# A macaron block on one core: row maxima five groups ahead instead of six, padded transposes later in their group, one first load of x

## The reference

```
x = x + 0.5 * ffn(layernorm(x))      # silu(x Wu^T) * (x Wg^T), then Wd^T; the three weights ternary
x = x + attn(layernorm(x))           # q, k, v with biases; causal softmax over 256 keys
x = x + 0.5 * ffn(layernorm(x))
```

## Time and profile before

| | us |
|---|---|
| runs | 593.73, 595.56, 595.39 (median 595.39) |
| the profiled execution, its own time | 593.51 |
| its span, first to last instruction | 591.8 |
| attention in it | about 200 to 424 |

### The profile page before, as it was taken

The page is one execution under the profiler, slowest core; times in us unless marked ns, Lnnn a source line. Parts: engine busy times, 40 slices in busy tenths (PEclk is TensorE's granted clock), DMA queues, the critical chain, the costliest instruction groups (busy, mean ns, idle before and its releaser), DMA issues.

```text
span 591.8 us, 12391 instructions
## 1 busy us (share of the span) xinstructions
PE 561.4 (95%) x4244; PEld 343.8 (58%) x4244; DVE 480.7 (81%) x1861; ACT 400.6 (68%) x717; POOL 169.3 (29%) x263
## 2 busy tenths in 40 slices
PE   2889999999999989999999999997999999999998
PEld 2345565655666755666566656554455665665566
DVE  5898978989875889898989897996797688756654
ACT  4857665674655378797888878886666665674642
POOL 3115201101530035454545454656401101100100
PEclk9999999999999999999999999999999999999999
DMA  8711101100105151423323323212201212111112
GB/s 297 229 34 37 18 19 37 36 19 19 37 18 126 39 112 56 93 78 71 88 64 101 76 74 84 66 50 39 37 1 35 64 45 69 39 55 54 35 37 72
DMA packets 72238, 37.90 MB, mean 64 GB/s; under 512 B 35536, under 2 KB 71632, under 8 KB 72144
## 3 DMA queue, kind: packets, MB, share of 16 engines
q1 hardware_dynamic: 72176, 37.11, 24.3%
HBM read 18.22 MB, written 10.49 MB: 49 GB/s over the span
## 4 chain that ended last, share of the span: by engine, by line
PE 71%; DVE 15%; DMA 4%; ACT 2%; issue 2%; SPq 2%; POOL 2%; DVEq 0%; ACTq 0%; POOLq 0%
PE bank L1163 33%; PE bank L1175 17%; DVE sm_out L980 6%; PE bank L1262 5%; PE bank L1319 4%; PE bank L1289 4%; PE bank L1330 4%; DMA q_st<-mx_hl 3%; PE bank L1335 2%; PE bank L1344 2%; DVE hid L849 1%; POOL xn L408 1%; DMA x<-in_x_dram 1%; DVE hl L864 1%; DVE stats L728 1%
## 5 line engine op out<-in xcount | busy, mean ns | idle before, releaser
L980 DVE CUSTOM_DVE_ANT_0 sm_out<-bank,mask 128x256 f16<-128x256 f32 (+1 forms) x512 | 151.3, 352 | 18.4 <-PE bank L1289 17.6
L481 ACT ACTIVATE silu<-bank,w_scale 128x512 f32<-128x512 f32 x128 | 87.3, 683 | 113.0 <-PE bank L1163 113.0
L849 DVE SCALAR_TENSOR_TENSOR hid<-silu,h_unit,bank 128x512 f32<-128x512 f32 x128 | 95.0, 743 | 63.8 <-ACT silu L481 63.5
L1175 PE MATMUL bank<-wT_down,hh 128*128 128x256 f16 x512 | 118.3, 273 | 2.5 <-DVE hl L864 2.3
L1175 PE MATMUL bank<-wT_down,hl 128*128 128x256 f16 x512 | 118.2, 273 | 0.0
L1163 PE MATMUL bank<-xh,wT_up 128*128 128x512 f16 x256 | 98.0, 383 | 1.0 <-DVE xl L793 0.7
L864 DVE TENSOR_TENSOR hl<-hid,hh 128x512 f16<-128x512 f32 x128 | 98.5, 770 | 0.0
L1163 PE MATMUL bank<-xh,wT_gate 128*128 128x512 f16 x256 | 97.3, 380 | 1.1 <-DVE hid L849 1.1
L1163 PE MATMUL bank<-xl,wT_up 128*128 128x512 f16 x256 | 98.0, 383 | 0.0
L1163 PE MATMUL bank<-xl,wT_gate 128*128 128x512 f16 x256 | 97.3, 380 | 0.0
L417 POOL TENSOR_TENSOR xnl<-xn,xnh 128x1024 f16<-128x1024 f32 x13 | 28.3, 2177 | 213.2 <-ACT xn L520 177.8
(11 more groups left out here) (133 smaller groups left out, 790.4 us busy)
## 6 DMA issues: line engine op xcount, KB each, us to landing
q_st<-q_scratch SPq DMA_DIRECT2D x32, 256.0 KB
q_scratch<-q_hl SPq DMA_DIRECT2D x16, 256.0 KB, 2.2
out_dram<-x SPq DMA_DIRECT2D x7, 512.0 KB, 3.0
x<-in_x_dram SPq DMA_DIRECT2D x1, 3072.0 KB, 15.5
k_scratch<-k_hl SPq DMA_DIRECT2D x16, 128.0 KB, 2.4
k_st<-k_scratch SPq DMA_DIRECT2D x16, 128.0 KB
shared<-in_w_up_t_dram SPq DMA_DIRECT2D x2, 512.0 KB, 6.7
shared<-in_w_gate_t_dram SPq DMA_DIRECT2D x2, 512.0 KB, 8.3
```

Source lines behind the costliest of these rows:

```text
L481: act.activation(silu[:, e % 2, :], U[e % 2][:, :], ACT.Silu, scale=w_scale[:, 0:1]).then_inc(silu_ready, 1)
L849: dve.scalar_tensor_tensor(out=hid[:, e % 4, :], in0=silu[:, e % 2, :], scalar=h_unit[:, 0:1], in1=GT[e % 2][:, :], op0=ALU.mult, op1=ALU. ...
L980: ins = dve.tensor_tensor_reduce(sm_out[:, i, cols], SM[i][:, cols], mask[:, S - size:S], -1.0 / MAX_UNIT, -MASKED, ALU.add, ALU.min, rowm ...
L1175: ins = pe.matmul(ACC[t % 2][:, 0:D], part[:, par, e, t * P:(t + 1) * P], wT_down[:, e, :], start=(e == 0 and part is hh), stop=(e == NE - ...
```

## The change

1. The lead is n + 5 where it was n + 6, on PE and on DVE. Before the loop, one group of row maxima fewer is made; in the last pair, one more.
2. `mx_q` is padded from 32 to 128 columns a half and cleared once at the start, and the transpose's stationary operand and its result are 128 wide. The copy reads the same 32 rows as before.
3. `max_transposes` moves from behind part 0 of `scores` to just ahead of part 2; `max_copy` from behind part 0 of `exps` to between parts 1 and 2; `max_parts` from ahead of `causal` to behind it.
4. Part 0 of `scores` of the groups 9, 17, 25, 33, 41, 49 and 57 (`n % 8 == 1`) is made one step early, ahead of `output_transposes`.
5. x's first chunk is loaded in one transfer instead of two.

```diff
-        mx_q = sb("mx_q", [P, 2, 2, HH, QT], F16)
+        mx_q = sb("mx_q", [P, 2, P], F16)
+        mx_parts = mx_q[:, :, 0:2 * HH * QT].rearrange("p n (a h t) -> p n a h t", a=2, h=HH)
-        MT = PV[0:2 * QT * HH, 0:P // 2].bitcast(F16)
+        MT = PV[:, 0:P // 2].bitcast(F16)
+        def begun_early(n):
+            return 2 < n < NG - 2 and n % 8 == 1
@@ sync
-            for half in range(2):
-                tiles = slice(half * TT // 2, (half + 1) * TT // 2)
-                sp.dma_start(x[:, tiles, :], x_dram[:, tiles, :]).then_inc(ld_x0[half], 16)
+            sp.dma_start(x[:, 0:TT, :], x_dram[:, 0:TT, :]).then_inc(ld_x0, 16)
@@ gpsimd, in attention_pair
-                        if g in (0, 2) and not end:
-                            max_parts(b + 1, g // 2)
                         if odd and g in (2, 3):
                             add_output(b - 1, g - 2, 3 - g)
                         if not (end and g == 3):
                             causal(4 * b + g + 1)
+                        if g in (0, 2) and not end:
+                            max_parts(b + 1, g // 2)
@@ scalar, in attention_pair
                             exps(n + 1, range(0, 1))
-                        if g % 2 and not end:
-                            max_copy(b + 1, g // 2)
                         if not last:
...
-                            exps(n + 1, range(1, 3))
+                            exps(n + 1, range(1, 2))
+                        if g % 2 and not end:
+                            max_copy(b + 1, g // 2)
+                        if not (end and g == 3):
+                            exps(n + 1, range(2, 3))
@@ vector
-                        lead = (4 * b + g + 6, (k + (g + 6) // 4) % 2, (g + 2) % 4)
-                        ahead = not (last and (k == 3 or (k == 2 and g >= 2)))
+                        lead = (4 * b + g + 5, (k + (g + 5) // 4) % 2, (g + 1) % 4)
+                        ahead = not (last and (k == 3 or (k == 2 and g == 3)))
...
-                for n in (4, 5):
-                    first_row_max(n)
-                row_max(6, 1, 2, 0)
+                first_row_max(4)
+                row_max(5, 1, 1, 0)
@@ tensor, in attention_pair
-                        if not (end and g == 3):
+                        if not (end and g == 3) and not begun_early(n + 1):
                             scores(*following, range(0, 1))
-                        if g % 2 and not end:
-                            pe.wait_ge(oT_ready, n)
-                            max_transposes(b + 1, g // 2)
...
                         projection(2)
+                        if g % 2 and not end:
+                            pe.wait_ge(oT_ready, n)
+                            max_transposes(b + 1, g // 2)
...
                             if not end:
-                                max_scores(n + 7, k + 2, 2, range(0, 1))
+                                max_scores(n + 6, k + 2, 1, range(0, 1))
+                                scores(*second, range(0, 1))
                             output_transposes(b, k, 0, (onorm_ready, 2 * b + 2))
@@ tensor, in attention
-                max_scores(5, 1, 1)
-                max_scores(6, 1, 2, range(0, 1))
+                max_scores(5, 1, 1, range(0, 1))
```

More of the change, by code:

```diff
@@ L133, in macaron_block @@
         LAST_ST = [SM[1], ST[0], ST[1]]
-        MT = PV[0:2 * QT * HH, 0:P // 2].bitcast(F16)
-        FIRST_MT = ST[0][0:2 * QT * HH, 0:P // 2].bitcast(F16)
+        MT = PV[:, 0:P // 2].bitcast(F16)
+        FIRST_MT = ST[0][:, 0:P // 2].bitcast(F16)
         ld_w = [[sem(f"ld_w{m}{half}") for half in range(2)] for m in range(3)]
-        ld_x0 = [sem(f"ld_x0{half}") for half in range(2)]
-        ld_x1, ld_xr = sem("ld_x1"), sem("ld_xr")
+        ld_x0, ld_x1, ld_xr = sem("ld_x0"), sem("ld_x1"), sem("ld_xr")
         xn_tile = sem("xn_tile")
@@ L346, in _ @@
             step(pool.tensor_copy(ident16[:, :], ident32[:, :]))
+            step(pool.memset(mx_q[:, :, :].bitcast(U32), 0))
             pool.memset(ones[:, :], 1.0).then_inc(const_ready, 1)
@@ L373, in max_parts @@
                 heads = rowmax[:, b % 2, :, half * HH:(half + 1) * HH].rearrange("p t h -> p h t")
-                pool.tensor_copy(mx_q[:, half, 0, :, :], heads).then_inc(mxhi_ready, 1)
+                pool.tensor_copy(mx_parts[:, half, 0, :, :], heads).then_inc(mxhi_ready, 1)
                 pool.wait_ge(mxhi_ready, 2 * b + half + 1)
-                pool.tensor_tensor(mx_q[:, half, 1, :, :], heads, mx_q[:, half, 0, :, :],
+                pool.tensor_tensor(mx_parts[:, half, 1, :, :], heads, mx_parts[:, half, 0, :, :],
                                    ALU.subtract).then_inc(mxlo_ready, 1)
@@ L583, in max_copy @@
                 maxima = FIRST_MT if b + half == 0 else MT
-                act.activation(mx_hl[:, half, :], maxima, ACT.Copy).then_inc(mx_ready, 1)
+                act.activation(mx_hl[:, half, :], maxima[0:2 * QT * HH, :], ACT.Copy).then_inc(mx_ready, 1)
             def exps(n, parts):
@@ L776, in ln_first @@
             def ln_first():
-                for half in range(2):
-                    dve.wait_ge(ld_x0[half], 16)
-                    ln_stats_of(0, range(half * TT // 2, (half + 1) * TT // 2))
+                dve.wait_ge(ld_x0, 16)
+                ln_stats_of(0, range(TT))
                 ln_moments(0)
@@ L1078, in attention_pair @@
                         if not (last and k == 3):
-                            row_max(4 * b + 10, (k + 2) % 2, 2, 0)
+                            row_max(4 * b + 9, (k + 2) % 2, 1, 0)
                         normalise(b, 0, 0)
@@ L1298, in max_transposes @@
                     pe.wait_ge(mx_ready, 2 * b + half)
-                pe.transpose(MT if b + half else FIRST_MT, mx_q[:, half, :, :, :].rearrange("p a h t -> p (a h t)"),
+                pe.transpose(MT if b + half else FIRST_MT, mx_q[:, half, :],
                              ident16[:, :]).then_inc(mxT_ready, 1)
@@ L1356, in attention_pair @@
                         n, end = 4 * b + g, last and k == 3
-                        lead = (n + 6, k + (g + 6) // 4, (g + 2) % 4)
-                        ahead = not (end or (last and k == 2 and g >= 2))
+                        lead = (n + 5, k + (g + 5) // 4, (g + 1) % 4)
+                        ahead = not (end or (last and k == 2 and g == 3))
                         def projection(place):
@@ L1363, in projection @@
                                 project(c + 2, at // 4, at % 4)
+                        second = (n + 2, b + (g + 2) // 4, k + (g + 2) // 4, (g + 2) % 4)
                         following = (n + 1, b + (g + 1) // 4, k + (g + 1) // 4, (g + 1) % 4)
                         if ahead:
-                            if g == 2:
+                            if g == 3:
                                 pe.wait_ge(st_loaded[1 - par][odd], 16 * N_ST * (pair + par + 1))
```

## The result

The changed kernel takes **609.38 us** (median of 4 runs, 607.93 to 610.57) against 595.45 for the kernel before in the same comparison: ratio 1.0237, 95% interval 1.0209 to 1.0265. It is slower, as forecast, but by 13.9 us where 6.6 was forecast (602 against 595.4), and outside the range of 590.5 to 607.

What follows compares the result with a forecast made beforehand. PE, DVE and ACT were taken as near full and tied by semaphores, DVE then transfers deciding even chunks, PE odd ones. -2.0 - 0.3 + 7.5 + 3.0 = +8.2 gave 602 us; own range 598.5 to 606, whole range 590.5 to 607.

Steps and rivals of the forecast that it cites:

- The prologue: Before the loop: one group of row maxima fewer lets the loop begin earlier, -2.0 us, between 0 and -2.2.
- The start: First load of x: one issue fewer sends the second chunk earlier, -0.3 us, between 0 and -0.5.
- The padding: At PE's 31 max transposes: the wider shape saves PE time but outputs then wait for ACT's copy, 0 us.
- what PE saves it waits: At the padded transposes: outputs wait for ACT's copy, so PE's saving from padding counts as 0.
- The copy, by its four places: The later ACT copy delays outputs in an odd chunk by 0.3, 0.5, 1.0 and 0.3 us.
- the 0.63 that the boundary was to hold: At an odd chunk's boundary: PE's 0.63 us of slack absorbs that much, leaving +2.0 of 2.6.
- The step that failed: Even chunks: only delay before DVE's gapless stretch, 0.3, and 0.2 at its other end count: +0.5 us each.
- The parts behind the masks: At g = 3 of an odd sequence: the transpose waits for POOL's later parts, +0.5 us, between 0 and 1.0.
- The last pair: Without projections PE reaches the waits sooner; a later load of maxima and later outputs cost +3.0 us, between 0 and 4.
- Early scores: At seven boundaries: scores begun early fill PE's wait for the results' copy, 0 us, at best -0.3 each.
- the wait for the copy is hidden: Rival for the late copy's places: its delays vanish, so the kernel is faster, 588.0 or 589.9 us; chance 0.17.
- under 0.7 us: Condition of the hidden-wait rival: it decides if an odd chunk's delay is under 0.7 us.

Runs made afterwards that it cites:

- the three small edits: Padded transposes, one first transfer of x and scores begun early; together, alone in the kernel before: 592.31 us, ratio 0.9953.
- the kernel with all three late places: The kernel before, lead still six, with the transposes, ACT's copy and POOL's parts at the changed kernel's late places: 611.69 us, ratio 1.0290.
- 631.8: The kernel before with only POOL's max_parts moved behind add_output and causal, transposes and copy early, lead six: 631.84 us, ratio 1.0625.
- 616.3: The changed kernel with POOL's max_parts put back ahead of add_output and causal, lead of five and late transposes and copy kept: 616.27 us, ratio 1.0363.
- 603.5: The changed kernel with ACT's copy ahead of part 1 of exps, still behind query_high, transposes left late: 603.46 us, ratio 1.0152.

## Why the prediction was right in sign and too small

From kernel to kernel the medians go +11.2 (copy), +0.4 (transposes), +6.0 (parts), -1.4 (the three small edits, from 611.69 to 610.28) and -0.9 (lead), together the 15.2 from 594.18 to 609.38 (13.9 against the 595.45 of its own comparison); the last two steps compare kernels that ran in different comparisons. In the profiles the difference of 17.0 was forecast as 8.2: -2.3 up to the first `outputs` (forecast -2.3), +4.9 for the three even chunks (forecast +1.5), +7.6 for the three odd ones (+6.0), +6.8 for the last pair (+3.0). Step by step:

- *The prologue, -2.0.* Right where it was read: the first x transposes at 210.0 against 212.1 with a lead of six, 2.1. But in the end only 0.9 is left in the medians. The group left out comes back in the last pair, where the prediction had DVE waiting: the first two `outputs` of the last chunk begin at 419.4 and 426.1 in after, at 421.0 and 426.9 with a lead of six, so that 2.1 became 1.6 and then 0.7. The chain of after runs over DVE there, through the row maxima of one group more, to the `scores` that wait for them (with a lead of six DVE is done with its maxima at 423.5, and the chain passes over PE):

```profile
423.91 0.20 DVE sm_out L984
424.11 0.02 DVE rowmax L984
424.13 0.14 issue
424.26 0.39 PE bank L1322
```

  These are single executions. Among kernels that are the same up to that point, the first `outputs` stand between 217.0 and 218.3, so tenths of such a difference mean little.
- *The start, -0.3.* Mechanism right. The statistics start 0.53 earlier in the profile; the whole kernel gains 0.8, with an interval from -0.2 to -1.4 that holds the forecast.
- *The padding, 0.* Wrong: it gives 2.0, or 1.4 at equal clock, with the places early. That 2.4 had been expected from 0.2 at four places of three odd chunks is near by luck, since the profile has the gain at one place of every chunk. So "what PE saves it waits" is not what happens. With the late places and a lead of six the small edits make the chunks 0.2 shorter too (29.9 for 30.1); what the padding alone gives there was not measured. The Trainium skill (TensorEngine Tiling (Array Packing), section Key Properties) says that a change of tiling mode drains TensorE. The traces agree as far as they go: PE's weight load stood at the narrow transpose for 9.5 us in 31, at the padded one for 2.2 in 5. Only a fraction of the 6.2 came back.
- *The copy, by its four places.* The shifts themselves were right. In chunk 3 of the kernel with the late copy, `outputs` start 8.2, 7.2, 5.5 and 8.5 apart, before 7.7, 6.2, 5.2 and 8.4: +0.5, +1.0, +0.3, +0.1, where +0.5, +1.0, +0.3 and +0.3 were forecast. The odd chunk cost 1.9 where the copy's share came to 1.5: the 0.63 that the boundary was to hold did not come off.
- *The step that failed* is the next one: "Of an even chunk: only what comes before DVE's unbroken stretch counts, 0.3, and some 0.2 at its other end: +0.5". With the copy late, an even chunk has the same +0.5 and +1.0 at the same two places and gets at most 0.7 back at the third (5.5 against 6.2, in chunk 2). It costs 0.8 to 1.5 by the copy alone, and in the changed kernel 1.4 in chunks 2 and 4 and 2.0 in chunk 0. DVE's unbroken stretch in the earlier trace rows was no wall behind which a late PE could hide: DVE takes `sm_out` from PE, and waits for it 33.5 us in after, 17.6 before. Both kinds of chunk together cost 12.5 where 7.5 was forecast.
- *The parts behind the masks, +0.5 at one place of an odd chunk.* Mechanism right, extent wrong: it costs 2.7 in the loop, in even chunks too (1.5 forecast), and 2.8 in the last pair, where groups are shorter and PE comes to each transpose before the parts are done. The chain of after there reads:

```profile
398.40 0.68 issue
399.08 0.23 PE bank L1302
399.33 0.28 ACT mx_hl L587
```

- *The last pair, +3.0.* It took 6.8 in the profiled execution. In the kernel with all three late places, at a clock of 1.00, it takes 3.9 more than before (+1.9 by the copy, -0.8 by the transposes, +2.8 by the parts). Most of the other 2.9 is the clock, and some the row maxima above:

```profile
420.00:424.00 4.00, 2.61 (x39) 1.36 (x28) 4.00 (x28) 2.35 (x4) 1.88 (x3) 1.00 0.33 74
424.00:428.00 4.00, 3.00 (x28) 1.40 (x32) 0.12 (x2) 1.98 (x4) 1.85 (x5) 0.61 0.30 67
428.00:432.00 4.00, 4.00 (x35) 1.61 (x31) 0.69 (x1) 1.88 (x3) 0.64 (x1) 0.53 0.00 0
432.00:436.00 4.00, 4.00 (x44) 1.98 (x37) 3.45 (x9) 2.76 (x6) 2.45 (x4) 1.00 0.00 0
```

  Two executions of the four had this (mean clock 0.994; 610.57 and 610.19), two did not (607.93 and 608.57): 2.1 us.
- *Early scores, 0.* Right.

Of the rivals, "the wait for the copy is hidden" is refuted by `outputs` that begin 0.06 us after the copy. The one of most use was its condition, "under 0.7 us": the kernel with the copy one instruction later meets it (0.2 in an odd chunk), and is 2.0 slower than before by the medians. The Trainium skill (Perfetto Trace Analysis, section Identifying the Most-Contended Engine) names the engine with the highest occupancy as the one to optimise first, with TensorE judged by MFU and by the busy share of its weight loads. By weight loads (58%) DVE, at 81%, would be that engine; yet the place of one 0.25 us copy on ACT, at 68%, costs 11.2.

What was missed altogether is that the late places are no free choices. That is shown for the transposes and the parts (631.8 and 616.3). No version with a lead of five was found that keeps the prologue's 2 us and loses nothing: the nearest is 603.5.

## What to carry to other kernels

When three engines are each over 80% busy and tied by semaphores, price a delay at each place where the next engine takes over with no slack, in every chunk, and take nothing off for a stretch in which another engine "sets the pace": it does so only until its supplier is later. Slack absorbs a small delay nearly whole and a larger one not at all: one more ACT instruction of 0.57 us ahead of the copy, at two places of a chunk, cost 0.6 us at equal clock and 2.0 by the medians; with an exponential more at all four places it was 11 us. Before moving producers closer to their use, follow the in-order queues behind them, as one order forces the next; and undo such a change edit by edit, for here the small edits alone were worth 2.8 us and lay hidden under it.

## What the runs showed of the hardware

The granted clock of TensorE fell in the last pair, after stretches in which PE was less busy. In the rows above it was 1.00 with PE busy for 2.61 of 4 us (2.40 in 416 to 420), then 0.61 and 0.53, close to the lower of its two levels, 1.2 GHz of 2.4, while PE worked on, and then 1.00 again. The kernel before does it too, more weakly: of the 25 executions beside the small edits 12 had a mean clock of 0.997 and a median near 595.3, the 13 at 1.00 one near 594.2. The kernel with the copy one instruction late lost its clock in 384 to 388 in the profiled execution:

```profile
380.00:384.00 4.00, 2.65 (x20) 1.73 (x19) 3.82 (x23) 2.22 (x5) 2.60 (x6) 1.00 0.78 170
384.00:388.00 4.00, 3.08 (x18) 1.40 (x22) 2.02 (x15) 1.94 (x4) 1.08 (x3) 0.62 0.03 7
```

PE's cover alone doesn't tell when it falls: the kernel with all three late places had PE busy for 6.27 and then 5.32 of 8 us in 416 to 432, and kept 1.00. So 1 to 2 us of a comparison of two such kernels can be the clock.
